# Layer 3 of a four-layer block: weight halves kept in DRAM instead of split again, and an order between VectorE and GpSimd in the values products

## The reference

```python
def _L3_cond_ref(x, router_logits, skill_gate, skill_up, skill_down, shared_gate, shared_up, shared_down):
    w, sel = top_k(softmax(router_logits), 2)           # per batch; w normalised
    out = sum over the two chosen skills of w * mlp(x, gate[e], up[e], down[e])
    return out + mlp(x, shared_gate, shared_up, shared_down)     # mlp: gelu(x@gate) * (x@up) @ down, 1024 hidden

def _L3_ffn_ref(x, ...):
    h = rmsnorm(x, gamma1); q = h @ Wq; k, v = split((h @ Wdown) @ Wup)
    att = einsum('bthd,btgd->bthg', q, k) / 4            # per token, 16 heads by 16 heads
    x = x + einsum('bthg,btgd->bthd', softmax(att), v) @ Wo
    h2 = rmsnorm(x, gamma2); gate = softmax(h2 @ Wg)
    return x + einsum('btd,edf,bte->btf', h2, We, gate)  # 8 experts
```

## Time and profile before

| | |
|---|---|
| median of 3 runs | 1498.51 us (1497.96 to 1502.99) |
| span of the profiled execution | 1512.8 us, mean granted clock 0.911 |
| that execution's own time | not recorded apart from the span |
| layer 3 in it | from 824 us on (batch 0 from 824.6, 1 from 918.2, 2 from 1045.9, 3 from 1209.5, tail from 1376) |
| PE, DVE, ACT, POOL busy | 87%, 68%, 39%, 47% |
| moved by DMA | 128.7 MB, mean 85 GB/s |

### The profile page before, as it was taken

The page is one execution under the profiler, slowest core; times in us unless marked ns, Lnnn a source line. Parts: engine busy times, 40 slices in busy tenths (PEclk is TensorE's granted clock), DMA queues, the critical chain, the costliest instruction groups (busy, mean ns, idle before and its releaser), DMA issues.

```text
span 1512.8 us, 18709 instructions
## 1 busy us (share of the span) xinstructions
PE 1310.2 (87%) x6536; PEld 1109.7 (73%) x6536; DVE 1030.2 (68%) x1854; ACT 591.9 (39%) x984; POOL 703.8 (47%) x371
## 2 busy tenths in 40 slices
PE   5998999999994899439888999988889979896698
PEld 4897787998783899427776888866677768774586
DVE  8599676498772655527756333589558973899987
ACT  3302423203312688415445545434543355342331
POOL 4320125520026577553004543587557655477790
PEclk9899999798986999759999999999999989996798
DMA  5300002300018799731001332222221212021000
GB/s 198 136 29 15 28 29 91 105 28 1 0 55 265 227 308 308 243 87 42 0 1 42 133 104 68 81 69 78 77 75 58 91 63 91 21 70 56 0 1 28
DMA packets 51772, 128.74 MB, mean 85 GB/s; under 512 B 6352, under 2 KB 30432, under 8 KB 51552
## 3 DMA queue, kind: packets, MB, share of 16 engines
q1 hardware_dynamic: 43840, 109.86, 22.4%
q0 software_dynamic: 4608, 12.59, 2.5%
q10 hardware_dynamic: 3232, 5.11, 1.0%
HBM read 105.25 MB, written 22.28 MB: 84 GB/s over the span
## 4 chain that ended last, share of the span: by engine, by line
PE 52%; DVE 16%; issue 10%; POOL 8%; ACT 4%; SPq 1%; another core or an unknown queue 1%; DMA 1%; POOLq 0%; DVEq 0%; ACTq 0%
PE bank L405 16%; PE bank L409 15%; PE bank L408 15%; POOL VW L458 4%; DVE bank L2343 2%; DVE G L458 1%; DVE F L2367 1%; DVE acc L2367 1%; POOL w_lo L593 1%; DVE acc L2636 1%; PE bank L955 1%; ACT w_hi L1603 1%; POOL w_lo L639 1%; POOL xs L601 1%
## 5 line engine op out<-in xcount | busy, mean ns | idle before, releaser
L405 PE MATMUL bank<-x_hi,w_hi 128*128 128x512 f32 (+1 forms) x560 | 221.2, 395 | 37.0 <-POOL w_lo L636 17.7
L636 POOL TENSOR_TENSOR w_lo<-raw,w_hi 128x1024 fp32r<-128x1024 f32 x48 | 117.9, 2456 | 226.9 <-ACT w_hi L1603 212.6
L408 PE MATMUL bank<-x_lo,w_hi 128*128 128x512 f32 (+1 forms) x560 | 214.5, 383 | 0.0
L409 PE MATMUL bank<-x_hi,w_lo 128*128 128x512 f32 (+1 forms) x560 | 213.9, 382 | 0.0
L405 PEld LDWEIGHTS bank<-x_hi,w_hi 128*128 128x128 f32 x560 | 111.6, 199 | 64.0 <-POOL w_lo L636 21.5
L405 PE MATMUL bank<-hid_hi,w_hi 128*128 128x512 f32 x328 | 131.8, 402 | 19.4 <-DVE hid_lo L2298 12.2
L1709 ACT ACTIVATE hid_hi<-bank 128x512 fp32r<-128x512 f32 x96 | 57.5, 599 | 195.9 <-DVE bank L2343 195.9
L409 PE MATMUL bank<-hid_hi,w_lo 128*128 128x512 f32 x328 | 129.6, 395 | 0.0
L408 PE MATMUL bank<-hid_lo,w_hi 128*128 128x512 f32 x328 | 129.5, 395 | 0.0
L409 PEld LDWEIGHTS bank<-x_hi,w_lo 128*128 128x128 f32 x560 | 110.9, 198 | 19.7
L408 PEld LDWEIGHTS bank<-x_lo,w_hi 128*128 128x128 f32 x560 | 111.6, 199 | 18.3
(11 more groups left out here) (473 smaller groups left out, 3636.6 us busy)
## 6 DMA issues: line engine op xcount, KB each, us to landing
raw<-in_skill SPq DMA_DIRECT2D x32, 768.0 KB
raw<-in_shared SPq DMA_DIRECT2D x16, 768.0 KB
raw<-in_l1e SPq DMA_DIRECT2D x20, 513.0 KB
base<-xs SPq DMA_DIRECT2D x38, 256.0 KB, 4.4
ys<-F SPq DMA_DIRECT2D x38, 256.0 KB, 4.9
VW<-in_l1e SPq DMA_DIRECT2D x18, 513.0 KB
raw<-in_l0c SPq DMA_DIRECT2D x12, 512.0 KB
raw<-in_qkv SPq DMA_DIRECT2D x8, 768.0 KB
```

The costliest lines, as they stand in the source:

```text
L405: i = nc.tensor.matmul(out, sh, mh, start=first, stop=False)
L408: nc.tensor.matmul(out, sh, ml, start=False, stop=False)
L409: return nc.tensor.matmul(out, sl, mh, start=False, stop=last)
L636: nc.gpsimd.tensor_tensor(lo[:, UP3], src[:, UP3], hi[:, UP3].bitcast(F32), ALU.subtract).then_inc(w_up_ready.sem, 1)
```

## The change

Two things:
- In a values half, GpSimd waits for VectorE's product of the same half.
- The order of chunks in a batch becomes shared 0, 1, 2, then the skills, then shared 3 (`ORDER3`). In batch 0 the shared chunks and the four expert chunks are split once, and SP stores both halves to DRAM (`keep`, `keep_special`). In batches 1 to 3 the shared chunks (12) are not split: two DMAs of 768 KB bring `hi` and `lo` straight into the slot (`kept3`), once TensorE is through with chunk n-3. Expert chunks come back the same way (`load_we`, 10 times 2 x 512 KB), the last two into the weight slots. `raw` counts only chunks that are split. All expert splits are in slots 12, 15, 18 and 21 of batch 0.

```diff
-EXPERTS3 = (2, 0, 1)
+SHARED3 = 2
+ORDER3 = ((2, 0), (2, 1), (2, 2), (0, 0), (0, 1), (0, 2), (0, 3), (1, 0), (1, 1), (1, 2), (1, 3), (2, 3))
+def kept3(n):
+    return n >= CHUNKS3 and ORDER3[n % CHUNKS3][0] == SHARED3
+WE_ORDER = (2, 3, 0, 1)
-SPECIALS = 2 + 4 * (BATCH - 1)
+SPECIALS = 2 + len(WE_ORDER)
+SPECIAL_SLOT = {4: 0, 9: 1, 12: 2, 15: 3, 18: 4, 21: 5}
+WE_LOAD_AT = {(2, 12): (0, 2), (2, 15): (0, 3), (3, 1): (1, 0), (3, 3): (1, 1), (3, 12): (1, 2), (3, 15): (1, 3),
+              (3, 19): (2, 0), (3, 21): (2, 1)}
...
+                j, c = ORDER3[n % CHUNKS3]
+                if kept3(n):
+                    sp.wait_ge(*d3_step(0, 2 * (n + 1 - W3_SLOTS)))
+                    sp.wait_ge(*kept_stored[c](0, 2))
+                    if n - W3_SLOTS in STORED3:
+                        sp.wait_ge(*kept_stored[ORDER3[n - W3_SLOTS][1]](0, 2))
+                    for dst, part in ((w_hi, 0), (w_lo, 1)):
+                        sp.dma_start(dst[n % W3_SLOTS][:].bitcast(F32), A["kept"][c, part]
+                                     ).then_inc(kept_in[n % W3_SLOTS].sem, 16)
+                    return
+                k = SPLIT3.index(n)
+                sp.wait_ge(*w_ready(0, CHUNKS + k + 1 - RAW_SLOTS))
...
+            def keep(n):
+                c = ORDER3[n][1]
+                sp.wait_ge(*w_ready(0, CHUNKS + SPLIT3.index(n) + 1))
+                for src, part in ((w_hi, 0), (w_lo, 1)):
+                    sp.dma_start(A["kept"][c, part], src[n % W3_SLOTS][:].bitcast(F32)
+                                 ).then_inc(kept_stored[c].sem, 16)
+            def keep_special(s):
+                c = WE_ORDER[s - 2]
+                sp.wait_ge(*s_ready(0, s + 1))
+                for src, part in zip(special(s)[1:], U):
+                    sp.dma_start(A["we_kept"][c, part], src.bitcast(F32)).then_inc(we_stored[c].sem, 16)
+            def load_we(p, c):
+                i = we_buffer(p, c)
+                sp.wait_ge(*we_stored[c](0, 2))
+                if i >= 2:
+                    sp.wait_ge(*d3_step(0, TILES3 * BATCH))
+                elif c < 2:
+                    sp.wait_ge(*we_ready(p - 1, 4 * c + 12))
+                else:
+                    sp.wait_ge(*we_ready(p, 4 * c - 4))
+                for dst, part in zip(we_at(i), U):
+                    sp.dma_start(dst.bitcast(F32), A["we_kept"][c, part]).then_inc(we_in[i].sem, 16)
...
             def dense_lo(n):
+                if kept3(n):
+                    return
...
+                if phase == "values":
+                    pool.wait_ge(*prod_dve(q, h + 1))
                 product3(nc.gpsimd, prod3_pool[h % 2], 2 + k, q % 2, phase, t).then_inc(prod_pool.sem, 1)
...
-            special_lo(10)
-            special_lo(11)
-            special_lo(12)
...
-            special_lo(13)
...
-                pe.wait_ge(*w_up_ready(0, n + 1))
+                pe.wait_ge(*(kept_here(n) if kept3(n) else w_up_ready(0, SPLIT3.index(n) + 1)))
...
             def dense_hi(n):
+                if kept3(n):
+                    return
```

More of the change, by code:

```diff
@@ L69, with we_buffer @@
 UP3, DOWN3 = slice(0, 1024), slice(1024, 1536)
-EXPERTS3 = (2, 0, 1)
+SHARED3 = 2
+ORDER3 = ((2, 0), (2, 1), (2, 2), (0, 0), (0, 1), (0, 2), (0, 3), (1, 0), (1, 1), (1, 2), (1, 3), (2, 3))
+PARTS3 = 4
+def kept3(n):
+    return n >= CHUNKS3 and ORDER3[n % CHUNKS3][0] == SHARED3
+SPLIT3 = [n for n in range(CHUNKS3 * BATCH) if not kept3(n)]
+KEPT3 = [n for n in range(CHUNKS3 * BATCH) if kept3(n)]
+STORED3 = [n for n in range(CHUNKS3) if ORDER3[n][0] == SHARED3]
+WE_ORDER = (2, 3, 0, 1)
+WE_BUFFERS = 4
 HALF_SLOT = [*range(10, 18), *range(20, 28)]
 WE_SLOT = [11, 12, 12, 13, 13, 14, 14, 15, 16, 16, 17, 18, 18, 19, 20, 20]
-SPECIALS = 2 + 4 * (BATCH - 1)
[L76 to L81, removed]
+SPECIALS = 2 + len(WE_ORDER)
+SPECIAL_SLOT = {4: 0, 9: 1, 12: 2, 15: 3, 18: 4, 21: 5}
+WE_LOADS = [(p, c) for p in range(BATCH - 1) for c in range(4) if not (p == 0 and c < 2)]
+WE_LOAD_AT = {(2, 12): (0, 2), (2, 15): (0, 3), (3, 1): (1, 0), (3, 3): (1, 1), (3, 12): (1, 2), (3, 15): (1, 3),
+              (3, 19): (2, 0), (3, 21): (2, 1)}
+def we_buffer(p, c):
+    return c if p == BATCH - 2 and c >= 2 else c % 2
 class Signal:
@@ L245, in build @@
         s_in, s_hi, s_ready = (sig("s_in", 0, 16), sig("s_hi", 0), sig("s_ready", 0))
+        tile_turns = [(TILES1 + 3 - i) // 4 for i in range(4)]
+        kept_stored, kept_in = (
+            [Signal(s.sem, 0, 16, prime=n) for s, n in zip(early, tile_turns)] for early in (y_out, xt_in))
+        we_stored = [Signal(s.sem, 0, 16, prime=n) for s, n in zip(
+            (*l0b_in, l1w_in, zeroed), (PAIRS, PAIRS, 1, ROUTED))]
+        we_in = [Signal(s.sem, 0, 16, prime=1) for s in x_in]
         d3_step = sig("d3_step", TILES3)
@@ L343, in special, with we_here, kept_here @@
                 return (640, 1024)[s], l3_hi[:, at], l3_lo[:, at]
[L344 to L351, removed]
-        def special_in(s):
[L355 to L359, removed]
+            return CWE, *we_at(WE_ORDER[s - 2] % 2)
+        def special_in(s):
+            return raw_s[:, 0:special(s)[0]], s_in(0, s + 1)
+        def we_here(p, c):
+            if (p, c) not in WE_LOADS:
+                return s_ready(0, 2 + WE_ORDER.index(c) + 1)
+            i = we_buffer(p, c)
+            turns = [pc for pc in WE_LOADS if we_buffer(*pc) == i]
+            return we_in[i](0, 2 * (turns.index((p, c)) + 1))
+        def kept_here(n):
+            turns = [k for k in KEPT3 if k % W3_SLOTS == n % W3_SLOTS]
+            return kept_in[n % W3_SLOTS](0, 2 * (turns.index(n) + 1))
         hrow = [G[u][:, 0:NT * D].rearrange("p (t d) -> p t d", t=NT) for u in U]
@@ new lines, in dense @@
+                k = SPLIT3.index(n)
+                sp.wait_ge(*w_ready(0, CHUNKS + k + 1 - RAW_SLOTS))
+                sp.dma_start(raw[k % 2][:], A["shared"][c] if j == SHARED3 else A["skill"][bass.ds(top3[j], 1), c]
+                             ).then_inc(raw_in[k % 2].sem, 16)
+            def keep(n):
[4 more added lines that the diff above has]
+                                 ).then_inc(kept_stored[c].sem, 16)
@@ L555, in _ @@
             dense(2, 0)
+            keep(0)
             for b in range(BATCH + 2):
@@ L679, in _ @@
                             half_sweep(p, h)
-                    if special_at(b, i) is not None:
-                        special_lo(special_at(b, i))
+                    if b == 0 and i in SPECIAL_SLOT:
+                        special_lo(SPECIAL_SLOT[i])
                     if i == 6 and 1 <= b < BATCH - 1:
@@ L1109, in l3_down @@
                 pe.wait_ge(*g3_hid(0, g + 1))
-                if ml == 0:
-                    pe.wait_ge(*w_ready(0, CHUNKS + n + 1))
+                if ml == 0 and not kept3(n):
+                    pe.wait_ge(*w_ready(0, CHUNKS + SPLIT3.index(n) + 1))
                 if i == 0 and b < 2:
@@ L1251, in last_experts @@
             def last_experts(p, n, c, t, dst):
[L1252 to L1253 removed]
+                wh, wl = we_at(we_buffer(LP, c))
+                pe.wait_ge(*we_here(LP, c))
                 for k in range(KD):
@@ L1715, in _ @@
                         finish3_after(p, i)
-                    if special_at(b, i) is not None:
-                        special_hi(special_at(b, i))
+                    if b == 0 and i in SPECIAL_SLOT:
+                        special_hi(SPECIAL_SLOT[i])
                     if i == 5 and 1 <= b < BATCH - 1:
```

72 lines of the change are left out of this document (41 added, 31 removed).

## The result

| | before | after |
|---|---|---|
| median of 8 runs each on one chip | 1498.03 us (1492.13 to 1503.24) | 1484.72 us (1478.77 to 1489.18) |
| span of the profiled execution, granted clock | 1512.8 us, 0.911 | 1481.6 us, 0.917 |
| layer 3 in it, first `gated` to the end | 688.2 us | 678.3 us |

The ratio is 0.9915 (95% interval 0.9892 to 0.9938), so 12.7 us, of 20.9 forecast. The two spans differ by 31 us, but 21.4 of that lies before layer 3, where nothing was changed: first `gated` at 824.64 and at 803.28.

A forecast was written before the change was run, and what follows sets the result against it. VectorE, with GpSimd behind it, was taken to bound the values slots; TensorE or latency the rest of batches 2 and 3. Terms of 6.5, 4.9, 1.5, 2.4, 6.7 less 1.1 gave 20.9 off 1498.5: 1477.6 us, range 1468 to 1489.

The forecast's parts named there:

- The mechanism: VectorE and GpSimd: instructions reading both inputs from SBUF run one after the other; VectorE's product 1.22 us undisturbed, up to 2.70.
- values slot: One hidden tile of a values phase, from its gated instruction: 5 to 7 us before, 4.65 forecast, VectorE the bound.
- batch 1 into 2: Values slots 21 to 4 across that turn: 41.0 us before, 34.5 after, gain 6.5.
- On SP a kept load waits for TensorE, and behind it stand the raw loads: SP's queue: raw chunks 15, 27 and 39 stand behind kept loads; chunk 15 hidden with 3 us to spare.
- the sum: All terms: 6.5 + 4.9 + 1.5 + 2.4 + 6.7 - 1.1 = 20.9 us off, giving 1477.6.
- batch 2 into 3: Values slots across that turn: 40.5 us before, 35.65 after, gain 4.85, taken as 4.9 in the sum.
- the scores: Batches 2 and 3: removed expert splits at slots 14 and 17 free products, 0.9 + 0.3, twice: gain 2.4.
- the tail: After batch 3: h_lo gains 2.1, the pair at 1414.69 ends earlier and two waits go; together 6.7 us.
- The kept load's own time: Loading a kept chunk of 1.57 MB: 0.9 + 4.6 + a little, 6 us, hidden with 2 us to spare.
- The pair left at 6.29: VectorE's tail pair at 1469.54, where GpSimd runs without a gap; left as is; rival "more" (0.12): up to 5.4 off.
- the value 0 for loads and stores that go strictly in order: Turn of batch 0: DMA cost between 0 (in order) and 4 us, taken as 1.1; at 0 the sum is 22.0.
- Absorbed: Rival, 0.15: TensorE or the gelu chain sets values slots at 5.2, tail gains only 2.1; 1487 to 1491 us.

## Why the prediction came out as it did

**The mechanism was right.** Two instructions that read both inputs from SBUF go one after the other, and the order between them decides. 4.65 us per values slot was forecast, 4.58 measured; batch 1 into 2 gained 6.0 of 6.5. Take the wait away and the product takes 3.1. The Trainium skill (SBUF - State Buffer, SBUF: two separate sides) calls the port pair of VectorE and GpSimd an exclusive lock that whoever starts first holds for the whole instruction; the 3.09 beside a GpSimd product that began 0.4 us earlier agrees (what was left of its 2.38, then some 1.1).

**The step of the prediction that failed: "On SP a kept load waits for TensorE, and behind it stand the raw loads".** The sentence named the raw loads and stopped there, so the sum has no term for the store. The output store stands behind the same load, one line further on in the queue's order, and ScalarE waits for it before it writes `base`. In the kernel before it stood behind a raw load that was fetched ahead. That made batch 2 into 3 +1.3 in place of -4.9; it cost 7.3 to 8.1 us by the runs with the store ahead. The step is 6.2 of the 11.1 us by which layer 3 misses the sum; the scores are 2.2, batch 1 into 2 0.5, the slots no term speaks of 5.6, and the tail with the slots before it gained 3.2 more than forecast. The kept load's own time was right (6 forecast, a median of 5.8 measured), and the raw loads were in time: ScalarE waits for none of them in layer 3. A queue that gets a new wait has to be read to its end, the stores too: for each DMA behind it, who waits for its landing.

**The term that was mis-sized: scores, 2.4 forecast, 0.2 measured.** The forecast took the expert split for what held VectorE's product of slot 15, though the earlier trace rows have it starting a microsecond after that product began. The split went, and the product still took 2.13, since GpSimd's own product, which comes late behind the weight split of its slot, holds it now as it did before. Even where the order frees part of it, the gain is 0.4 us per batch. The first to suspect is the instruction that was running when the slow one began.

**The tail was right**, 7.7 against 6.7 to the gate work, and each half of it was shown alone. The pair left at 6.29 stayed. The 1.5 us gained behind the gate work, where 0 was forecast, come with the removed splits: from the gate work to the end it is 85.3 us before, 85.5 with the wait alone, 83.8 without the tail's splits and 83.8 in the changed kernel. By what wait was not looked at.

**The small terms.** TensorE waits 0.7 us in slot 1 of batch 1 for a kept load behind the stores of batch 0, and the slot takes 1.0 more, of 1.1 forecast (1.0 to 1.9 more in the other kernels with the same loads there). So the value 0 for loads and stores that go strictly in order was not met. The slots that no term speaks of lost 5.6. Slot 2 of batch 0 has 1.6 of it: 2.54 in the one profile of the kernel before, but 4.17 and 4.14 in its two variants (wait alone, tail's splits left out), 5.36 without the wait and 4.11 to 4.16 in all others. So the change isn't what made it longer. Most of the rest are slots that come in steps from run to run: slot 10 of batches 2 and 3 took 10.84, 12.48 or 13.7 us with unchanged code. It was 10.85 and 12.47 before, 12.49 and 13.76 after.

**Slips that changed nothing.** 20.9 - 9 - 4.6 is 7.3 and not 7.5. A raw chunk of 0.79 MB from 896.9 to 899.6 is a mean of 290 GB/s; 350 is the fullest microsecond of it.

**Rivals.** Absorbed was the likeliest of them and its number (1487) is not far from the result, but by another mechanism: the slots did reach 4.58 and the pair did fall. The result near that number comes of the store and the scores, so it is a coincidence and no confirmation. For the rest of the sum the runs with the store ahead speak: 0.9847 and 0.9862 are 21 to 23 us of 1498, close to the 20.9. That is in part luck too, as the tail's excess of 3.2 stands there against the 2.2 of the scores.

## What to carry to other kernels

When a load on an in-order queue gets a wait on compute, list every DMA behind it and the consumer of each, output stores above all, and put those whose data is ready ahead of it. Freeing an engine doesn't pay by itself: here it paid only together with an order between the two engines, and without that order it cost 0.4%. When a slow instruction is put down to a neighbour, check by the start times which instruction of the neighbour was running when the slow one began, and what stands next in its queue, before the gain is booked.

## What the runs showed of the hardware

- VectorE's pair with both inputs in SBUF waited through the rest of one and two more whole GpSimd instructions that followed each other without a gap (5.9 us for the first of the pair), and got in only when GpSimd was idle. Where GpSimd stood still at the end of one instruction, the pair took 1.74. But VectorE isn't always passed over: in slot 15 of batch 2 of the kernel before, its product got in at 1152.88, between GpSimd's product and the split behind it, and the split took 3.40 in place of 2.3; of the pair at 1414.69 the first took 2.90, between the split (ended 1417.04) and the next product. What decides was not found out.
- A 512 KB store issued 0.5 us behind 1.5 MB of loads on the same queue landed some 7.7 us after issue (1188.47 to ScalarE's start at 1196.21), the two later ones in 2.6. With the store ahead of that load it took 6.7, and in the kernel before 5.3. Stores of 768 KB, two issued one after the other, landed in a median of 7.4 and 9.0 us, loads of the same size in 4.3 and 5.8.
- The same slot of unchanged work takes different time in one execution. Windows over slot 10 of batches 2 and 3 in the second run with the store ahead (PE, PEld, DVE, ACT, POOL, then the granted clock):

```profile
1085.50:1099.30 13.80, 13.80 (x62) 12.31 (x61) 3.63 (x5) 5.98 (x8) 8.18 (x4) 0.64 0.16 57
1246.40:1257.30 10.90, 10.90 (x62) 9.55 (x62) 3.64 (x5) 5.98 (x8) 8.23 (x4) 0.84 0.22 74
```

62 matmuls in both, the mean granted clock 0.64 and 0.84 of 2.4 GHz: 2.9 us for a slot. What tips it was not found out; any single profile's slots 2, 4, 10 and 12 are uncertain by that much.
